# A merged attention and feed-forward pipeline laid out anew: loads by need, denominators at the head of a period, both reciprocals beside the numerators, one router block per slot

## The reference

```python
# layer 0, attention part (AFT with a local band), per batch
emb = layernorm(x) + ctx
q, k, v = emb @ wq + bq, emb @ wk + bk, emb @ wv + bv
w  = pos_bias * (abs(i - j) < 64)
ek, ew = exp(k - max_k), exp(w - max_w)
num, den = ew @ (ek * v), ew @ ek
y  = sigmoid(q) * num / den
a  = layernorm(y @ wo + bo + emb) * gamma + beta
part = layernorm(relu(a @ w1 + b1) @ w2 + b2 + a) * gamma + beta
# layer 0, feed-forward part: mixture of 64 experts, 8 of them chosen, and 2 shared ones
probs = softmax(xf @ router_w + router_b); tw, ti = top_k(probs, 8); tw = tw / sum(tw)
routed = sum over experts of cw * (silu(xf @ W1 + B1) @ W2 + B2)
```

## Time and profile before

| what | value |
|---|---|
| median of 3 runs | 1273.25 us (1272.36 to 1275.16) |
| the profiled execution's own time | 1272.18 us |
| its span in the profile | 1270.5 us |
| TensorE busy (matmuls) | 1142.3 us, 90% of the span |
| VectorE, ScalarE, GpSimd busy | 878.1, 703.6, 343.7 us |
| first period (hidden(0)) begins | 92.3 us |
| periods 1 to 6 begin | 146.4, 203.6, 256.2, 291.7, 326.0, 360.4 us |
| first hidden tile of the next phase | 400.9 us |

### The profile page before, as it was taken

How to read it: one execution, slowest core, us unless ns; L and a number is a source line. 1 busy time by engine, 2 the same in 40 slices (tenths; PEclk the granted TensorE clock), 3 DMA queues, 4 the chain that set the end, 5 groups by cost and what they waited for, 6 DMA issues and landing times. The chain is left out here.

```text
span 1270.5 us, 19924 instructions
## 1 busy us (share of the span) xinstructions
PE 1142.3 (90%) x6928; PEld 997.4 (79%) x6928; DVE 878.1 (69%) x1653; ACT 703.6 (55%) x1063; POOL 343.7 (27%) x343
## 2 busy tenths in 40 slices
...
PEclk9989999899998999999999999999999999998999
...
GB/s 313 67 1 1 1 1 1 1 1 137 71 71 112 113 115 138 94 120 134 91 95 54 1 76 100 100 58 59 136 64 54 138 62 119 95 39 5 14 24 48
DMA packets 68967, 92.88 MB, mean 73 GB/s; under 512 B 16016, under 2 KB 33168, under 8 KB 68752
## 3 DMA queue, kind: packets, MB, share of 16 engines
...
## 5 line engine op out<-in xcount | busy, mean ns | idle before, releaser
L1997 DVE CUSTOM_DVE_ANT_0 at_pr<-at_sc,at_mk 128x512 f32<-128x512 f32 x256 | 165.5, 683 | 26.2 <-PE at_sc L2228 25.7
L1901 ACT ACTIVATE at_pr<-at_pr,at_nmx 128x512 f32<-128x512 f32 x256 | 170.5, 717 | 17.8 <-DVE at_nmx L1997 17.2
L2139 DVE TENSOR_TENSOR W_1l<-at_pt,W_1h 128x1024 fp32r<-128x1024 f32 x128 | 155.8, 1218 | 6.1 <-ACT W_1h L1896 5.7
L1896 ACT ACTIVATE W_1h<-at_pt 128x1024 fp32r<-128x1024 f32 x128 | 130.8, 1022 | 34.7 <-PE at_o L2262 33.2
L2243 PE MATMUL at_pt<-ident,at_pr 128*128 128x128 f32 x1024 | 135.2, 275 | 15.0 <-DVE W_1l L2139 14.2
L2243 PEld LDWEIGHTS at_pt<-ident,at_pr 128*128 128x128 f32 x1024 | 115.3, 142 | 38.4 <-issue 17.0
L228 ACT ACTIVATE moe_hs<-moe_hid,cols 128x512 f32<-128x512 f32 x120 | 82.8, 690 | 100.4 <-PE moe_hid L114 99.5
L247 DVE TENSOR_TENSOR moe_hl<-moe_ms,moe_hh 128x512 fp32r<-128x512 f32 x104 | 80.4, 773 | 64.3 <-ACT moe_hh L220 64.3
L261 DVE TENSOR_TENSOR moe_ms<-moe_hs,gate 128x512 f32<-128x512 f32 x104 | 78.7, 757 | 57.4 <-ACT moe_hs L228 57.0
L220 ACT ACTIVATE moe_hh<-moe_ms 128x512 fp32r<-128x512 f32 x104 | 65.8, 633 | 94.2 <-DVE moe_ms L261 94.2
L2262 PE MATMUL at_o<-W_1h,at_vaug 128*128 128x512 f32 x256 | 112.1, 438 | 0.3 <-DVE W_1l L2139 0.3
...
## 6 DMA issues: line engine op xcount, KB each, us to landing
gate<-expert_weights SPq DMA_DIRECT2D x256, 128.0 KB, 3.0
w_stage<-in_ew SPq DMA_DIRECT2D x32, 256.0 KB, 4.0
at_kp<-at_heads SPq DMA_DIRECT2D x96, 64.0 KB, 2.7
at_qp<-at_heads SPq DMA_DIRECT2D x96, 64.0 KB, 2.8
w_stage<-in_mask SPq DMA_DIRECT2D x16, 256.0 KB, 3.6
at_rb<-at_recip SPq DMA_DIRECT2D x64, 64.0 KB, 2.1
w_stage<-in_w SPq DMA_DIRECT2D x8, 256.0 KB, 7.3
w_stage<-in_sw SPq DMA_DIRECT2D x8, 256.0 KB, 3.3
```

Source lines behind the costliest of these rows:

```text
L1896: act.activation(PH[0][:, n % 2, :], PT[n % 2][:, :, :].rearrange("p c q -> p (c q)"), ACT.Copy)\
L1901: act.activation(pr_of(t)[:, x, :], pr_of(t)[:, x, :], ACT.Exp, bias=nmx[:, t % 4, x:x + 1], scale=-1.0).then_inc(s["ex"], 1)
L1997: dve.tensor_tensor_reduce(pr_of(t)[:, x, :], SB[x][:, :], mk[u // 2 % 2][:, j, :], -float(HD) ** -0.5, 3.0e38, ALU.add, ALU.min, nmx[:, t ...
L2139: dve.tensor_tensor(PH[1][:, n % 2, :], PT[n % 2][:, :, :].rearrange("p c q -> p (c q)"), f(PH[0][:, n % 2, :]), ALU.subtract).then_inc(s[ ...
```

## The change

The work is the same; its order on the queues, and what some of it waits for, differ:
- **Loads.** ScalarE's queue issues the four weights before pos. ident, cols and rows have a semaphore each, and each user waits for its own. The weights are rounded and subtracted in four parts, in the order k, v, q, o.
- **Start.** key(0) and value(0) come before the transposes of exp(pos) (`turn_ew`), in pairs around query(0). denominators(0) precedes turn_emb(1). `emb_bias` is split from `emb_apply` and comes later. turn_ek(1), denominators(1), ek_low(1), den_times(1) and emb_apply(2) move from period 0 into the start.
- **Banks.** From batch 1 on, the transposed keys and the denominators use XB (`key_banks`), not YB; logits use R[0] and turn_logits R[1], not R[2] and R[3]; biases instead of logits wait for add_bias (`s["out"]`). turn_emb(b) for b >= 2 waits for den_times(b - 1).
- **Periods.** turn_ek of the next batch moves to slot 7, before turn_z; denominators open the next period; turn_ekv, numerators go one slot earlier (1 and 2); both reciprocals are in slot 2, make_y and y_low in slot 3; exp_k in slot 3, exp_q heads slot 7, weighted in slot 5, emb_stats in slot 4; turn_z in slot 7; z_high and z_low in slot 0 of the next period.
- **Router.** turn_weights and biases come behind output in slots 6 and 7; ScalarE's weights and centre for the new x in slot 7, after relu and high; the stats of the new x in slot 6, not 4; turn_low at the head of slot 1.
- **GpSimd.** The betas are added in pairs behind the numerators of batches 1 and 2; root_emb precedes root_z.

The diff without the new names, bank arguments and waits listed above (indentation shortened):

```diff
 sp.dma_start(g.attn[:, 0:TT, :], ctx[:, 0:TT]).then_inc(af["ctx"], 16)
-sp.dma_start(g.cols[:, :], a["cols"]).then_inc(g.consts, 16)
-sp.dma_start(g.ident[:, :], a["ident"]).then_inc(g.consts, 16)
+sp.dma_start(g.ident[:, :], a["ident"]).then_inc(af["id"], 16)
+sp.dma_start(g.cols[:, :], a["cols"]).then_inc(af["cols"], 16)
...
 group_split(pool, g, 0)
-root_z(0)
-add_b2(0)
-root_emb(2)
-add_beta(0)
-add_beta(1)
-root_z(1)
-add_b2(1)
-root_emb(3)
-add_beta(2)
-root_z(2)
-add_b2(2)
-add_beta(3)
+for b in range(B - 1):
+  if b:
+    pool.wait_ge(af["num"], 2 * b + 2)
+    for k in (2 * b - 2, 2 * b - 1):
+      add_beta(k)
+  if b + 2 < B:
+    root_emb(b + 2)
+  root_z(b)
+  add_b2(b)
 pool.wait_ge(s["sum"], 1)
...
       low_group1(j)
+  if b == 0:
+    root_z(3)
   root(b, 1, s["mv2"], s["eps2"], s["root2"], s["sh2"])
   if b == 0:
-    root_z(3)
     add_b2(3)
...
-act.dma_start(pos[:, :, :], a["pos"].rearrange("(t p) n -> p t n", p=P)).then_inc(af["pos"], 16)
 for j, n in enumerate(("wq0", "wk0", "wv0", "wo0")):
   act.dma_start(wst[:, j], a[n].rearrange("(c p) n -> p c n", p=P)).then_inc(af["w"], 16)
+act.dma_start(pos[:, :, :], a["pos"].rearrange("(t p) n -> p t n", p=P)).then_inc(af["pos"], 16)
 act.wait_ge(af["w"], 64)
-act.activation(W[0][:, :, :, :], wst, ACT.Copy).then_inc(af["wh"], 1)
+for j in (1, 2, 0, 3):
+  act.activation(W[0][:, j, :, :], wst[:, j], ACT.Copy).then_inc(af["wh"], 1)
...
+def ew_high(jc):
+  act.wait_ge(af["ewt"], jc + 1)
+  act.activation(ewT[0][:, jc, :], YB[jc % 2][:, :], ACT.Copy).then_inc(af["ewh"], 1)
...
+emb_high(0)
 act.wait_ge(af["npm"], 1)
...
   act.activation(pos[:, tt, :], pos[:, tt, :], ACT.Exp, bias=npm[:, tt:tt + 1]).then_inc(af["ew"], 1)
-emb_high(0)
-for jc in range(TT):
-  act.wait_ge(af["ewt"], jc + 1)
-  act.activation(ewT[0][:, jc, :], YB[jc % 2][:, :], ACT.Copy).then_inc(af["ewh"], 1)
 exp_k(0)
+ew_high(0)
+ew_high(1)
 exp_q(0)
+ew_high(2)
+ew_high(3)
+ek_high(0)
+emb_high(1)
 act.wait_ge(s["w"], 32)
...
 act.activation(B2[0][:, :], b2s[:, :], ACT.Copy).then_inc(s["wh"], 1)
-ek_high(0)
-emb_high(1)
 ekv_high(0)
...
 exp_q(1)
+ek_high(1)
 z_high(0)
...
     n = i * SLOTS + t
-    if turned < B:
-      if t == 1:
+    if t == 0 and 1 <= i < B:
+      if turned < B:
         ek_high(turned)
-      if t == 3:
-        ekv_high(turned)
-      if t == 7:
-        z_high(turned)
+      z_high(i)
+    if turned < B and t == 2:
+      ekv_high(turned)
+    if early < B and t == 7:
+      exp_q(early)
     if n < LAST:
       relu(n)
+    if turned < B and t == 3:
+      y_high(turned)
     if 1 <= n <= LAST:
...
       continue
-    if early < B:
-      if t == 1:
-        emb_high(early)
-      if t == 2:
-        exp_k(early)
-    if turned < B and t == 4:
-      y_high(turned)
-    if early < B and t == 6:
-      exp_q(early)
+    if early < B and t == 1:
+      emb_high(early)
+    if early < B and t == 3:
+      exp_k(early)
     if i == B - 1 and t < 4:
...
       exponentials(i - 3)
-    if t == 6:
+    if t == 7:
+      if i >= 3:
+        weights(i - 3)
       if 2 <= i <= B + 1:
...
         centre(i - 2, 1, x_of(i - 2), xn, s["sh2"], s["tx"], C, s["xn"])
-      if i >= 3:
-        weights(i - 3)
...
+def ew_low(jc):
+  dve.wait_ge(af["ewh"], jc + 1)
+  dve.tensor_tensor(ewT[1][:, jc, :], YB[jc % 2][:, :], f(ewT[0][:, jc, :]), ALU.subtract).then_inc(af["ewl"], 1)
...
 dve.wait_ge(af["x"], 16)
...
 dve.wait_ge(af["ctx"], 16)
-dve.wait_ge(g.consts, 48)
 emb_apply(0)
+for k, j in enumerate((1, 2, 0, 3)):
+  dve.wait_ge(af["wh"], k + 1)
+  dve.tensor_tensor(W[1][:, j, :, :], wst[:, j], f(W[0][:, j, :, :]), ALU.subtract).then_inc(af["wl"], 1)
+emb_low(0)
+dve.wait_ge(af["cols"], 16)
 dve.tensor_scalar(nbq[:, :], g.cols[:, col_at("bq0"):col_at("bq0") + C], -1.0, None, ALU.mult)\
  .then_inc(af["nbq"], 1)
+dve.wait_ge(af["band"], 2)
+dve.tensor_reduce(npm[:, :], pos[:, :, :], AX.X, ALU.max, negate=True).then_inc(af["npm"], 1)
+dve.wait_ge(af["nbq"], 1)
+k_max(0)
+weighted(0)
+ew_low(0)
+ew_low(1)
 dve.wait_ge(af["rest"], 32)
 emb_stats(1)
-dve.wait_ge(af["nbq"], 1)
-dve.wait_ge(af["band"], 2)
-dve.tensor_reduce(npm[:, :], pos[:, :, :], AX.X, ALU.max, negate=True).then_inc(af["npm"], 1)
-dve.wait_ge(af["wh"], 1)
-dve.tensor_tensor(W[1][:, :, :, :], wst, f(W[0][:, :, :, :]), ALU.subtract).then_inc(af["wl"], 1)
-emb_low(0)
+ew_low(2)
+ew_low(3)
+ek_low(0)
+dve.wait_ge(g.consts, 16)
+emb_bias(0)
 emb_apply(1)
-for jc in range(TT):
-  dve.wait_ge(af["ewh"], jc + 1)
-  dve.tensor_tensor(ewT[1][:, jc, :], YB[jc % 2][:, :], f(ewT[0][:, jc, :]), ALU.subtract).then_inc(af["ewl"], 1)
-k_max(0)
-weighted(0)
-ek_low(0)
+den_times(0)
 emb_low(1)
-den_times(0)
+emb_bias(1)
 invert(0, 0)
...
 invert(0, 1)
+emb_stats(2)
 make_y(0)
 y_low(0)
+ek_low(1)
+z_stats(0)
 weighted(1)
-z_stats(0)
-emb_stats(2)
 z_scaled(0)
+den_times(1)
+z_low(0)
+emb_apply(2)
 dve.wait_ge(s["wh"], 2)
...
 dve.tensor_tensor(B2[1][:, :], b2s[:, :], f(B2[0][:, :]), ALU.subtract).then_inc(s["wl"], 1)
-z_low(0)
 dve.wait_ge(s["wl"], 2)
...
     n = i * SLOTS + t
-    if turned < B:
-      if t == 1:
+    if t == 0 and 1 <= i < B:
+      if turned < B:
         ek_low(turned)
-      if t == 2:
-        den_times(turned)
-      if t == 3:
-        ekv_low(turned)
-      if t == 4:
-        make_y(turned)
-      if t == 5:
-        z_stats(turned)
-      if t == 7:
-        z_low(turned)
+      z_low(i)
+    if t == 1 and 3 <= i < B + EARLY:
+      turn_low(i - 3)
     if t == 2 and 1 <= i <= B:
...
       add_expert_y(i - B - 1)
+    if turned < B:
+      if t == 1 and i:
+        den_times(turned)
+      if t == 2:
+        ekv_low(turned)
+      if t == 3:
+        make_y(turned)
+      if t == 5:
+        z_stats(turned)
     if FIRST <= n < LAST:
...
     if turned < B:
-      if t in (2, 3):
-        invert(turned, t - 2)
-      if t == 4:
+      if t == 2:
+        invert(turned, 0)
+        invert(turned, 1)
+      if t == 3:
         y_low(turned)
...
     if early < B:
-      if t == 0:
+      if t == 0 and i:
         emb_apply(early)
...
       if t == 4:
+        emb_bias(early)
+        if early + 1 < B:
+          emb_stats(early + 1)
+      if t == 5:
         weighted(early)
-      if t == 7 and early + 1 < B:
-        emb_stats(early + 1)
-    if t == 1 and i >= 3:
-      turn_low(i - 3)
     if t == 2 and 2 <= i <= B + 1:
...
       new_x(i - 2)
-      stats(i - 2, 1, x_of(i - 2), s["new"], i - 1, s["bn2"], s["mv2"])
     if t == 5 and i >= 3:
       normalise(i - 3)
+    if t == 6 and 2 <= i <= B + 1:
+      stats(i - 2, 1, x_of(i - 2), s["new"], i - 1, s["bn2"], s["mv2"])
...
   pe.wait_ge(s["cwTs"], b + 1)
+  if b:
+    pe.wait_ge(s["out"], 2 * b)
   for tt in range(TT):
...
     pe.wait_ge(af["ek"], 2 * b)
-  if b >= 3:
-    pe.wait_ge(af["e"], 2 * b)
+  if b >= 2:
+    pe.wait_ge(af["dm"], 2 * b)
   for c in range(C):
...
     pe.wait_ge(af["e"], 2 * b)
+  else:
+    pe.wait_ge(af["wl"], 3)
   project(0, q_banks(b), af["q"])
...
-def turn_keys(src, done):
+def turn_keys(src, banks, done):
   for jc in range(TT):
...
-pe.wait_ge(g.consts, 48)
-turn_emb(0)
-pe.wait_ge(af["ew"], TT)
-for jc in range(TT):
+def turn_ew(jc):
+  pe.wait_ge(af["ew"], TT)
   if jc >= 2:
...
   last.then_inc(af["ewt"], 1)
-pe.wait_ge(af["wl"], 1)
...
+pe.wait_ge(af["id"], 16)
+turn_emb(0)
 key(0)
 value(0)
+turn_ew(0)
+turn_ew(1)
 query(0)
+turn_ew(2)
+turn_ew(3)
 turn_ek(0)
+denominators(0)
 turn_emb(1)
-denominators(0)
+turn_ekv(0)
 key(1)
-turn_ekv(0)
 value(1)
 numerators(0)
+query(1)
+turn_ek(1)
 project_out(0)
-query(1)
+denominators(1)
 turn_z(0)
...
     n = i * SLOTS + t
+    if t == 0 and i and turned < B:
+      denominators(turned)
     if n < LAST:
...
         turn_logits(i - 3)
+    if 2 <= n < LAST + 2:
+      output(n - 2)
+    if turned < B:
+      if t == 1:
+        turn_ekv(turned)
+      if t == 2:
+        numerators(turned)
+      if t == 4:
+        project_out(turned)
+      if t == 7:
+        if early < B:
+          turn_ek(early)
+        turn_z(turned)
+    if 3 <= i < B + EARLY:
       if t == 6:
...
         biases(i - 3)
-    if 2 <= n < LAST + 2:
-      output(n - 2)
-    if turned < B:
-      if t == 0:
-        turn_ek(turned)
-      if t == 1:
-        denominators(turned)
-      if t == 2:
-        turn_ekv(turned)
-      if t == 3:
-        numerators(turned)
-      if t == 4:
-        project_out(turned)
-      if t == 6:
-        turn_z(turned)
...
```

More of the change, by code:

```diff
@@ L481, in early_phase @@
     s = {n: sem("fr_" + n) for n in names}
-    names = ("x", "ctx", "rest", "pos", "w", "wh", "wl", "pow", "band", "npm", "ew", "ewt", "ewh", "ewl", "nbq",
+    names = ("x", "ctx", "id", "cols", "rest", "pos", "w", "wh", "wl", "pow", "band", "npm", "ew", "ewt", "ewh", "ewl", "nbq",
              "es", "em", "ev", "er", "ea", "et", "ab", "ett", "eth", "etl", "k", "v", "q", "km", "kb", "nb", "ek", "e", "ekv",
@@ L728, in logits @@
                     act.wait_ge(s["lt"], b)
```

(7 more changed lines are left out.)

37 lines of the change are left out of this document (21 added, 16 removed).

## The result

The changed kernel takes 1243.22 us (median of 4 runs, 1240.03 to 1244.7); the kernel before, on the same chip, 1274.2 us (4 runs, 1272.36 to 1276.89). The ratio is 0.975, 95% interval 0.9731 to 0.9768: 31 us less. The profiled execution took 1242.67 us, with a span of 1240.9. The forecast was 1241, out of a sum of 32; so the interesting part is whether the terms are right.

What follows compares the result with a forecast made beforehand. TensorE, busy 90% of 1270.5 us, bounds the kernel, so gains in the first 400 us arrive whole. Terms 16+8+1+1.5+3.5+0+2 = 32 off 1272.2 give 1240.2, median 1241; range 1231 to 1250, with rivals 1228 to 1260.

Steps and rivals of the forecast that it cites:

- The start: Stretch up to hidden(0): key(0) at about 18 us, not 43.4, hidden(0) at 76, not 92.3; 16 us gained.
- three heads of line: In the start: emb_apply(0) behind the constants' rows, W's rounding behind weights landing after pos, npm behind emb_stats(1); all removed.
- Period 0: 43.4 us of work plus waits at query(2), value(2), denominators(2) and clock: 46.5 against 54.1 us, 8 gained (5 to 9).
- Period 1: 49 us of work, new 3.3 us wait at turn_emb(3) for den_times(2), 1.7 for lower clock: 56.4 against 57.2, 1 gained.
- Period 2 and the entry to 3: Small waits, then hidden(24) 7 us late because z_high(3) stands behind centre: 51 against 52.6 us, 1.5 gained (-2 to 5).
- Periods 3 to 5: Router periods: first 32 against 35.5 us, 3.5 gained; next two sum 0, one output earlier against apply_gate(32) 2 us late.
- Period 6 and the end: Last router period up to the next phase, with no centre or new x in the way: 2 us gained (0 to 4).
- the same two edits give 2: Period 6: output ahead of turn_weights and stats in slot 6, as priced in period 3, gain 2 us (0 to 4).
- The page on transposes: Ahead of each denominators: transposes don't count as busy for the clock gate, so low clock three times, 5 us more, 1246.
- Late chains cost twice: Late gates, z_high behind centre, den_times behind emb_apply cost double: +4, +7, +3 us, so 1255 us; chance 0.16.
- The clock takes it back: Changed stage: many short waits each draw half clock, 78 us more of it, costing 39, so 1280 us; chance 0.05.
- Nearly all waits go: Periods 0 to 2: TensorE needs only 43.4, 49 and 38 us plus 4; gain 32+12, so 1229 us; chance 0.10.

Runs made afterwards that it cites:

- the third single edit: Changed kernel with all four turn_ew ahead of key(0) on TensorE again, ScalarE's and VectorE's order to match: 1250.42 us, ratio 0.9795.
- all three moves: Changed kernel with ScalarE's weights copies in slot 6, centre of the first new x behind z_high(3), denominators(2) behind hidden(8): 1225.89 us, ratio 0.9618.

## Why the prediction was right, point by point

**The start** was right by its steps: key(0) forecast at about 18, came at 17.53; npm done at 23.4, was at 23.7; turn_ew(0) 26.0, was 26.31; hidden(0) 76, was 75.51. Two of the three heads of line that I named were undone by themselves, the weights behind pos (2.2 us) and emb_stats(1) before npm (5.6); the third, the wait for the rows, only together with others, and the 6.5 us of the third single edit are TensorE's own order. They aren't additive. For emb_apply(1), and the 3.77 us above agree with the rule of the Trainium skill (SBUF — State Buffer, Who interferes with whom) that the engine which comes second to the shared ports blocks; the same four parts took 1.38 us at 8.92, where GpSimd was idle.

**Period 0** came out right (45.8 for 46.5), but the sums under it don't add up: its terms give 47.6, not 46.5, those of period 1 57.4, not 56.4, and those of period 3 31.2, not 32. Added as written, the whole gain is 30 and the time 1243. (And denominators are 24 matmuls of 512 columns, not 48; the 5.6 us are right.) One gain the forecast didn't price: emb_apply(2) took 5.2 us at 93.0 in the kernel before, beside GpSimd's add_beta, and 1.4 at 75.3 now that the betas come later. No run undid that move.

**Period 1**: the forecast 3.3 us at turn_emb(3) was 3.05, and moving denominators(2) took it away. For that wait I also gave 1.7 us to the lower clock. In this trace it didn't fall (1.00 from 126.9 to 181.5), which is most of why period 1 came out 1.8 shorter. But in the second trace of the very same kernel it did, behind the same wait:

```profile
133.89 1.88 PE L1220 MATMUL rt_r<-ident,aft_emb 128*128 128x128 f32 x8 [3.04 <-DVE aft_sg L981]
```

Eight transposes took 1.88 us there and not 1.06, an output's matmuls of 256 columns stood 0.21 apart and not 0.12, the mean clock from 126.5 to 181.5 was 0.97, and period 1 took 56.1 us. So the term was not wrong; it comes in one execution and not in the other. hidden(24), behind 6.9 us, began with a matmul pitch of 0.43 us, the lower level, in both.

**Period 2 and the entry to 3**: the 7 us at hidden(24) were 6.94. The small waits around it were smaller than given (output(18) 2.2 for 2.7, output(20) 0.3 for 1.0, turn_z 0.8 for 1.3).

**Periods 3 to 5** were right: 3.4 and 0.5 for 3.5 and 0. apply_gate(32), forecast 2 us late, came 5.2 after hidden(32), where relu alone would allow 3.1. The "0" was a balance of a real gain (turn_weights no longer waits) and a real loss (gates late); the run with the copy in slot 6 takes only the loss away, and periods 4 and 5 are 4.2 us shorter.

**Period 6 and the end** is the term that failed: -4.3 for +2. The step is "the same two edits give 2": the forecast carried its gain into period 6, but not the late gate and the late copy that it had priced in periods 4 and 5, and it didn't follow the last copy to the end of the stage. That end shows how it counts. SyncE's store of the last `cwo` was issued 34.8 us into period 6 (360.34) and the next phase began 10.0 later; with weights in slot 6 and with all three moves the first figure is 32.9 and 30.9, and the second 9.9 both times. So in the new layout the end of the stage hangs on that copy, store and eight gate issues. Before, the store came 28.6 us into the period and the next phase 11.8 behind it, presumably because TensorE's last output (397.45) came behind the last gate issue (396.19). 6.2 us later, less 1.9, is the 4.3.

Of the 6.2 us, the traces put 4.0 ahead of the router's weights, which VectorE has ready 30.8 us into the period (26.8 before), and 2.1 between them and the store, where turn_weights now stands behind an output and the copy behind relu and high. The run with the copy in slot 6 gives back 1.9 of the whole. Two things lie ahead of these weights and can each add to the 4.0. The first gate product begins 4.8 us into the period, not 2.3, as its gate is late. And the split of group 2, which I had costed at nothing because it ends in time, now runs from 4.8 to 23.7 us into the period (330.3 to 349.2); before, it ran from 3.6 us ahead of the period to 15.1 into it (356.8 to 375.5). It makes what runs on VectorE slow: without it f_hl takes 0.68 us on average, with it 1.09 (with the three moves 0.81 and 1.06). The page named above also says that a VectorE instruction with two SBUF inputs contends with a GpSimd instruction that reads SBUF, and the two groups of lines agree.

But this slowness isn't new. The same two groups in period 6 of the kernel before:

```profile
L824 DVE TENSOR_TENSOR f_hl<-f_hs,f_hh 128x512 fp32r<-128x512 f32 x10 | 10.5, 1054 | 0.1
L831 DVE TENSOR_TENSOR f_hs<-f_hs,gate 128x512 f32<-128x512 f32 x8 | 6.2, 777 | 11.2 <-ACT f_hs L653 11.2
```

So the 4.3 us that the period loses with its split in the new layout aren't the price of the change: the old layout had the split beside the same products and took 40.5 us with it. What differs is where in the period it runs. Now it also covers `choose` (its last step took 1.36 us, before 0.42), on the way to the router's weights. No run took the split out of the kernel before or put it back to its old place in the new one, so how the 4.0 us divide between the late gate and the later split stays open.

**The hit on the total** has some luck in it. Period 6 was off by 6.3 us, and the start and periods 0 to 2 together gained about 5 more than forecast. And of the 31 us only 9.8 were undone by a run. The gains of periods 0 to 3, about 18 us, are read from waits that are gone from the trace, and no experiment takes them back one by one.

**The page on transposes** (the Trainium skill, TensorE: Matmul & The Clock Gate, Part 4) would have had the lower level ahead of each denominators. Here turn_ek and turn_z (from 118.78 on), a 0.76 us wait and denominators(2) follow one another, and from the second matmul on the pitch is 0.23 us, full clock:

```profile
121.34 0.50 PE L114 MATMUL rt_r<-W_1h,aft_kTh 128*128 128x512 f32 x1 [0.76 <-DVE aft_kTl L970]
121.68 0.39 PE L114 MATMUL rt_r<-W_1h,aft_kTl 128*128 128x512 f32 x1
121.91 0.40 PE L114 MATMUL rt_r<-W_1l,aft_kTh 128*128 128x512 f32 x1
```

It is the same at 175.89. The 5 us that the rule would add were not there; whether transposes count in longer stretches, no run shows.

**The rivals.** "Late chains cost twice" fell for z_high and den_times, which cost what they were given; the late gates and copy cost 2 us more than that, in period 6. "The clock takes it back" fell: 29 us at the lower level from 17.5 to the next phase (33 in its second trace), 41 in the kernel before. That is under a tenth of the stage, the forecast's own mark, though not by much. "Nearly all waits go" didn't happen in the changed kernel. But the three moves, which are three of the waits that this forecast had named, bring 1225.9, below the range given for the change.
